# Two layers of cross attention on Trainium2: norm products in place, earlier first loads, clears shared out by layer, and a new order of the steps

## The reference

```python
# layer 0
text_out = softmax(q k^T / 4) v                  # q = x Wq, k and v from the 77 tokens
# four tokens ip = context[77:], none here: a softmax over no tokens adds nothing
x = text_out Wo + bo + x
# layer 1: text = context[:73], ip = context[73:77]
probs_t  = softmax(q k_t^T / 4)                  # over 73 tokens
text_out = probs_t v_t
qsem     = l2norm(probs_t @ text)                # 512 wide, for each head and query
sem      = qsem @ l2norm(ip)^T
fused    = q k_ip^T / 4 + 0.5 * sem
ip_out   = (softmax(fused) * spatial_mask) v_ip
x = (text_out + ip_out) W_out + b_out + x
```

## Time and profile before

| | |
|---|---|
| median of three runs | 2631.1 us (2628.68 to 2633.44) |
| the profiled execution | 2627.46 us, span 2625.7 us |
| busy share of the span | TensorE 89%, VectorE 66%, ScalarE 66%, GpSimd 60% |
| mean granted clock of TensorE | 0.976 of full |
| what ended last, by engine | TensorE 32%, DMA 15%, SyncE's queue 14%, ScalarE 10%, GpSimd 8% |
| first phase | 0 to 340.22 us |
| second phase | 340.22 us to the end |

### The profile page before, as it was taken

How to read it: one execution, slowest core, us unless ns; L and a number is a source line. 1 busy time by engine, 2 the same in 40 slices (tenths; PEclk the granted TensorE clock), 3 DMA queues, 4 the chain that set the end, 5 groups by cost and what they waited for, 6 DMA issues and landing times.

```text
span 2625.7 us, 90322 instructions
## 1 busy us (share of the span) xinstructions
PE 2329.1 (89%) x35896; PEld 1455.7 (55%) x35896; DVE 1724.0 (66%) x3053; ACT 1728.2 (66%) x2602; POOL 1580.1 (60%) x1055
## 2 busy tenths in 40 slices
PE   7899937989989999998999899999999999899984
PEld 5677724555555555555555555555555555555542
DVE  5533323777777777777777777777777777677764
ACT  3332315777777777777777777777777777777762
POOL 3121024666677666666666667777676666676663
PEclk9999968999999999999999999999999999999996
DMA  8667622343434433334334344334444343434331
GB/s 274 201 211 224 195 82 58 100 110 108 110 102 110 111 106 105 110 108 112 104 109 110 107 109 111 108 107 111 110 112 111 98 112 106 110 106 111 105 90 53
DMA packets 337021, 310.90 MB, mean 118 GB/s; under 512 B 179440, under 2 KB 280048, under 8 KB 336624
## 3 DMA queue, kind: packets, MB, share of 16 engines
q1 hardware_dynamic: 336624, 305.35, 41.6%
HBM read 164.66 MB, written 105.98 MB: 103 GB/s over the span
## 4 chain that ended last, share of the span: by engine, by line
PE 32%; DMA 15%; SPq 14%; ACT 10%; POOL 8%; issue 5%; DVE 3%; ACTq 0%; POOLq 0%; DVEq 0%
PE psum L927 12%; DMA rb<-r_dram 8%; DMA den<-ust 6%; SPq L854 6%; PE psum L1010 5%; ACT ef L1115 5%; PE psum L991 4%; POOL ust L1297 4%; PE psum L1024 4%; POOL al L1302 4%; SPq L861 3%; ACT ah L1153 2%; PE psum L930 2%; SPq L881 1%; ACT ust L1123 1%
## 5 line engine op out<-in xcount | busy, mean ns | idle before, releaser
L1115 ACT ACTIVATE ef<-psum 73x1024 f32<-73x1024 f32 (+1 forms) x640 | 636.9, 1015 | 266.1 <-PE psum L994 248.1
L1335 POOL TENSOR_TENSOR e<-ef,eh 73x1024 f32<-73x1024 f32 x320 | 681.9, 2131 | 81.5 <-ACT eh L1130 81.4
L1176 DVE TENSOR_REDUCE mneg<-psum 128x8 f16<-128x584 f32 (+1 forms) x640 | 464.2, 775 | 105.9 <-PE psum L959 91.5
L1198 DVE TENSOR_TENSOR wr<-psum,e 73x1024 f32<-73x1024 f32 x320 | 390.3, 1220 | 163.6 <-PE psum L1024 160.6
L991 PE MATMUL psum<-q_high,keys 32*73 32x256 f16 (+2 forms) x6144 | 323.8, 258 | 63.1 <-ACT ust L1123 32.0
L1010 PE MATMUL psum<-ef,values 128*32 128x256 f32 x5120 | 357.9, 388 | 4.4 <-DVE wr L1198 4.0
L1024 PE MATMUL psum<-eh,gram 128*73 128x512 f16 x1280 | 338.5, 387 | 12.9 <-ACT ef L1115 11.3
L1297 POOL TENSOR_TENSOR ust<-ust,rb 128x768 f32<-128x768 f32 x128 | 231.7, 1810 | 186.4 <-DMA rb<-r_dram 185.9
L1130 ACT ACTIVATE eh<-ef 73x1024 f16<-73x1024 f32 x320 | 315.6, 1045 | 0.0
L1123 ACT ACTIVATE ust<-psum 128x512 f32<-128x512 f32 x384 | 229.2, 597 | 122.7 <-PE psum L1010 121.9
L991 PEld LDWEIGHTS psum<-q_high,keys 32*73 32x73 f16 (+1 forms) x6144 | 187.6, 110 | 158.4 <-ACT ust L1123 45.5
(11 more groups left out here) (162 smaller groups left out, 4553.5 us busy)
## 6 DMA issues: line engine op xcount, KB each, us to landing
rb<-r_dram SPq DMA_DIRECT2D x128, 384.0 KB, 4.1
keys<-k_dram SPq DMA_DIRECT2D x128, 231.0 KB, 2.8
values<-v_dram SPq DMA_DIRECT2D x128, 192.5 KB
x<-in_x SPq DMA_DIRECT2D x64, 384.0 KB, 3.6
ust<-ust SPq DMA_DIRECT2D x512, 48.0 KB, 2.1
v_dram<-vst SPq DMA_DIRECT2D x16, 1280.0 KB
out<-outt SPq DMA_DIRECT2D x64, 320.0 KB, 3.2
k_dram<-kst SPq DMA_DIRECT2D x32, 616.0 KB, 4.0
```

Source lines behind the costliest of these rows:

```text
L1115: act.activation(ef[l][0:m, unit_heads(n), :].rearrange("t h s -> t (h s)"), src, ACT.Exp, scale=SM).then_inc(s_exp[l], 1)
L1176: dve.tensor_reduce(dst, o, AX_X, ALU.max, negate=True).then_inc(s_max[l], 1)
L1198: dve.tensor_tensor(wr[0:m, k % LOW_RING, :, :].rearrange("t (r h) s -> t r (h s)", r=2), banks(l, f"u{k}", 2)[0:m, :, :], e2[0:m, k % LOW ...
L1335: pool.tensor_tensor(e2[0:m, k % LOW_RING, :, :], ef[1][0:m, unit_heads(k), :], eh[0:m, unit_heads(k), :], ALU.subtract).then_inc(s_e2, 1)
```

## The change

1. **Norm products in place.** The tile `wr` is gone. `e2` has five buffers instead of three, and VectorE's `w` writes its product over the rest that it read. GpSimd's `b` for a batch waits for TensorE's `n` of the batch before (`f_n`), where it waited for `w` and a ring.
2. **First loads within the first phase.** The constants, the first input `x`, the layer 0 keys of batch 0 and the high and low parts of that input are made in the first phase, in tiles that both phases share (`Early`). To make room the raw projection weights take the place of `raw_v0` and `raw_v1`, and are loaded after the weights have been split.
3. **Stores of values in pieces.** Each of the five pieces of 128 (the last 104) rows is stored by itself as soon as it is ready, with one semaphore for each layer.
4. **Clears shared out by layer.** `all_ready` is gone. Small clears, clears for layer 0 and clears for layer 1 have a semaphore each, and only the steps of the first batch that need them wait.
5. **New orders.** All five lists of `ORDER`, and `USES`, are new.

```diff
+        small_clears, dve_clears, pool_clears = [mneg[0], mneg[1], va[0], va[1], gm], [ef[0]], [ef[1], eh, e2]
...
-        def all_ready(eng):
-
-            eng.wait_ge(s_zero, CLEARED)
-            eng.wait_ge(s_w, 16 * CONSTANTS)
...
             def weighted(l, b, k):
-                b.reached(dve, f_n, UNITS, k + 1 - LOW_RING if k >= LOW_RING else (4, 5, 3)[k] - UNITS)
                 b.reached(dve, s_e2, UNITS, k + 1)
                 b.reached(dve, f_u, UNITS, k + 1)
...
+                rest = e2[0:m, k, :, :].rearrange("t (r h) s -> t r (h s)", r=2)
+                dve.tensor_tensor(rest, banks(l, f"u{k}", 2)[0:m, :, :], rest, ALU.mult).then_inc(s_wr, 1)
...
             def rests(l, b, k):
-                b.reached(pool, s_wr, UNITS, k + 1 - LOW_RING if k >= LOW_RING else (4, 5, 3)[k] - UNITS)
+                b.reached(pool, f_n, UNITS, k + 1 - UNITS)
...
                 for l in both:
-                    results_of("v", l, 0)
-                    dst = v_dram[l][bass.DynSlice(token, full * P), :].rearrange("(k p) n -> p k n", p=P)
+                    for c, (k0, m) in enumerate(VT):
+                        wait_taken(sp, b, slot, KV_USES.index(("v", l, c, 0)))
+                        dst = v_dram[l][bass.DynSlice(token + k0, m), :]
...
+            for t, d in constants:
+                sp.dma_start(t[:], d).then_inc(s_const, 16)
+            sp.dma_start(early.xin[:], x[0:1, :, :, :].rearrange("a c p s -> p (a c) s")).then_inc(early.s_x, 16)
...
+            sp.wait_ge(s_kstored[0], 16 * KSTORES * 2 * (PAIRS - 1))
+            sp.dma_start(early.ke[:], k_dram[0][0:1, :, :].rearrange("a p n -> (a p) n")).then_inc(early.s_ke, 16)
...
             def exponentials(l, b, n):
+                if first(b):
+                    act.wait_ge(s_zero[l], CLEARED[l])
```

More of the change, by code:

```diff
@@ L1 @@
 from contextlib import ExitStack
+from dataclasses import dataclass
 import numpy as np
@@ L283, in keys_and_values @@
         s_kstored = [sem(f"keys_stored{half}") for half in (0, 1)]
-        s_istored, s_gstored, s_vstored = sem("ip_keys_stored"), sem("gram_stored"), sem("values_stored")
+        s_istored, s_gstored = sem("ip_keys_stored"), sem("gram_stored")
+        s_vstored = [sem(f"values_stored{l}") for l in both]
         s_ghigh = sem("gram_high")
@@ L317, in load_projection @@
             def load_projection(n):
+                sp.wait_ge(s_wl, len(order))
                 if n >= 2:
                     sp.wait_ge(s_pl, n - 1)
[L321 removed]
+                sp.dma_start(rawp[n % 2], projections[n][0].rearrange("(k p) n -> p k n", p=P))\
                   .then_inc(s_rawp[n % 2], 16)
@@ L401, in _ @@
             sp.wait_ge(s_last, 96)
+            sp.wait_ge(s_const, 16 * len(constants))
+            sp.wait_ge(s_keyless, 1)
             for half in (0, 1):
@@ L405, in _ @@
             sp.wait_ge(s_gstored, 16 * 2 * 2 * PAIRS)
-            sp.wait_ge(s_vstored, 16 * VSTORES * 2 * PAIRS)
+            for l in both:
+                sp.wait_ge(s_vstored[l], 16 * VSTORES * 2 * PAIRS)
         @block.tensor
@@ L656, in _, with attention @@
             pairs(pool, chunk)
-def attention(nc, psum, x, mask, bias, ident16_d, sel_d, pick_d, kmask_d, vmask_d, k_dram, v_dram, g_dram, c_dram,
-              kip_dram, vip_dram, r_dram, n_dram, s_dram, p_dram, wqs, wos, wqt, wot, rnorm, out):
+            pool.wait_ge(early.s_x, 16)
+            pool.tensor_copy(early.xh[:], early.xin[:]).then_inc(early.s_xh, 1)
+            pool.wait_ge(early.s_xh, 1)
+            pool.tensor_tensor(early.xl[:], early.xin[:], early.xh[:], ALU.subtract).then_inc(early.s_xl, 1)
+def attention(nc, psum, early, x, k_dram, v_dram, g_dram, c_dram, kip_dram, vip_dram, r_dram, n_dram, s_dram, p_dram,
+              wqs, wos, wqt, wot, rnorm, out):
     both = (0, 1)
@@ L690, in attention @@
         ql = [sb(f"q_low{l}", [P, PW], F16) for l in both]
-        ke = [sb(f"keys{l}", [P, 2 * CW * 2 * T], F16) for l in both]
+        ke = [early.ke, sb("keys1", [P, 2 * CW * 2 * T], F16)]
         va = [sb(f"values{l}", [P, H, SLOT]) for l in both]
@@ L807, in load_keys @@
             def load_keys(l, b, n):
+                if l == 0 and first(b):
+                    return
                 b.reached(sp, f_t[l], CW, 0)
@@ L812, in load_values @@
             def load_values(l, b, n):
+                if first(b):
+                    sp.wait_ge(s_small, SMALL)
                 b.reached(sp, f_a[l], CW, 0)
@@ L1167, in maxima @@
                 m = TXT[l]
+                if first(b):
+                    dve.wait_ge(s_small, SMALL)
                 b.reached(dve, f_m[l], 1, 0)
@@ L1279, in _ @@
         def _(pool):
+            for t in small_clears:
+                pool.memset(t[:], 0.0).then_inc(s_small, 1)
             for t in pool_clears:
-                pool.memset(t[:], 0.0).then_inc(s_zero, 1)
-            all_ready(pool)
+                pool.memset(t[:], 0.0).then_inc(s_zero[1], 1)
             def high_input(l, b, n):
+                if l == 0 and first(b):
+                    return
                 b.reached(pool, f_q[l], 1, 0)
@@ L1339, in _ @@
                                    "at": text_attended, "al": low_attended, "c": sem_values, "kb": ip_keys, "vb": ip_values, "b": rests})
+@dataclass
+class Early:
+    ident16: object
+    sel: object
+    pick: object
+    kmask: object
+    vmask: object
+    mask: object
+    bias: list
+    kip: object
+    xin: object
+    xh: object
+    xl: object
+    ke: object
+    s_x: object
+    s_ke: object
+    s_xh: object
+    s_xl: object
 def attention_stack_kernel(nc, x, ctx, ctxip, mask, wq, wk, wv, wo, bias, wk_ip, wv_ip, ident16_d, sel_d, pick_d,
```

139 lines of the change are left out of this document (67 added, 72 removed), and 16 rows, old and new, of the table USES.

## The result

The changed kernel takes 2531.36 us (median of four runs, 2517.18 to 2539.48) against 2629.89 us for the kernel before, measured beside it: a ratio of 0.9618, 95% interval 0.9573 to 0.9664. Measured once more (experiment 1), it gave 0.9597 (0.958 to 0.9613). The forecast was 2519 us, with a range of 2458 to 2588.

A forecast was written before the change was run, and what follows sets the result against it. It took a 33.97 us period, closed by the chain from denominators to 0o plus TensorE's work, as the bound. 91 us from 62 periods plus 21 at the boundary gave 112 us, so 2519 us, range 2458 to 2588.

The forecast's parts named there:

- Boundary: Between the two phases: earlier first projection and earlier block start together gain 21 us, bounds 18.2 to 22.2.
- that term: TensorE's clock after the boundary: a shorter gap could keep 2.4 GHz and save 6.5 us once; left out of the sum.
- Steady part: The loop over batches: the period falls from 33.97 to 32.5 us, bounds 31.5 to 33.6, 91 us over 62 periods.
- third cycle: TensorE's work alone in a period: 31.2 us, and nothing is faster than that.
- rival (a): TensorE becomes the only bound, the norm chain being shorter: period 31.5 us, time about 2457 us; chance 0.17.
- The jitter: Average period over the closely read one: 0.6 us before, 0.2 us added after, for a slow DMA partly covered by other chains.
- The small waits: TensorE's waits for two maxima and for the exponential, about 0.3 us each, beside the norm chain and not on top.
- First cycle: Denominators to 0o: 1.84 us of SyncE's queue leaves the chain, which falls from 19.35 to 17.6 us; whole cycle 31.5 us.
- Second cycle: Norms through DRAM, roots, 1o, w1 and VectorE's 0o: a 12.4 us chain against 11.3 of TensorE's work; binds at 32.3 us.
- (b): The new orders give nothing, only the boundary is won: period 33.9 us, time 2606 us; chance 0.09.
- my own case: Boundary gain plus a period of 32.5 us: 2519 us, own range 2463 to 2590; chance 0.69.
- (c): Slower: SyncE's queue becomes the bound through the input `x`; at a period of 34.7 us the time is 2655; chance 0.05.

The follow-up runs named there:

- experiments 2 and 3: The clamp of the norms written to PSUM and copied from there: in the changed kernel 2520.07 us (0.9567), in the kernel before a ratio of 0.9957.
- experiment 7: The kernel before with only SyncE's queue shortened, the stores and loads between the denominators' steps moved behind them: 2575.34 us against 2618.66, ratio 0.9833.
- experiment 6: The changed kernel with Gram matrix and key loads and the scores' store put back behind the inverses' stores on SyncE's queue: 2592.1 us, ratio 0.9835.
- experiment 10: The changed kernel with VectorE's 1o ahead of the roots and the clamp of the norms written to PSUM: 2583.51 us, ratio 0.9861 to the kernel before.
- experiment 11: The changed kernel with the clamp of the norms in PSUM and TensorE's 1a1 ahead of 1u2: 2527.73 us, ratio 0.9653 to the kernel before.
- experiment 5: The changed kernel with the five order lists and the bank order of the kernel before, everything else kept: 2612.36 us, ratio 0.9917.
- experiment 9: The changed kernel with VectorE's 1o ahead of the first root step instead of behind six: 2719.99 us, ratio 1.0321 to the kernel before.
- experiment 4: The changed kernel with the clamp of the norms as an instruction with two float32 inputs in SBUF: 2526.41 us, ratio 0.9576 to the kernel before.

## Why the prediction came out as it did

**Boundary: right.** 21 us forecast; the first projection comes 22.0 us earlier and the first read of 0o 20.6, since the way between the two takes 1.4 us longer. The block starts 2.9 us earlier (2.7 forecast, by the store in pieces), and the projection 0.2 us behind it (0 to 1.1). The three clears of GpSimd took 13.1 us beside other work, as forecast. VectorE's clear stands in the chain at 338.46 for 4.33 us, beside the projection, as the price said: the first `q_low`, ready to start when ScalarE ends `q_high` at 342.33, follows the clear at 342.70, so it cost 0.4 us at most. The clock averaged 0.58 and 0.66 instead of 0.50, so the shorter stand did not keep 2.4 GHz, and leaving that term out was right. The 6.5 us that I had worked out beside the Trainium skill, "TensorE: Matmul & The Clock Gate", Part 1, did not come in a size that the times show.

**Steady part: direction right, size a little off.** 1.47 us a period forecast (91 us in 62; there are 63), 1.21 measured (76.2 in 63). The forecast was 31.2 us of work and 1.3 of waits; it came to 30.73 and 2.03. Three terms were mis-sized and partly cancel:
- TensorE's own work. I took the same set of steps to mean the same busy time. The norm sums put together take 0.48 us less. The floor of 31.2, on which the third cycle and rival (a) rested, was not a floor. That the total still came out near is partly luck: this error and the next two pull opposite ways.
- The jitter. I added 0.2 us for it. The mean stands 0.35 over the median (32.74 and 32.39), and I had the wrong picture of its cause: not a slow DMA in one of several tight chains, but VectorE's clamp held up by GpSimd. It was already there in the kernel before, where the shortest and the longest clamp took 0.19 and 2.16 us; experiments 2 and 3 took it out in both kernels, for 8 and 11 us, through 0o in the one and through 0t0 in the other.
- The waits of a period without jitter. I had 1.1 us, by the norms' cycle alone; the median period has 1.66 (32.39 less 30.73). The small waits, which I took to lie beside that cycle and left out of the sum, are the larger part of it: the hand-offs below.

**First cycle: right for before, its new length not tested alone.** The wait for `al` went from 56.9 us to 11.5. That it bound the old period is shown by experiment 7. The forecast that it leaves the bound after the change holds too: even with 1.84 us of queue put back, `al` is waited for only 4 times. What I missed is that the edit of the queue works on both cycles: keys stood behind `rw`, and the norms hang on keys (experiment 6).

**Second cycle: the place right, the 12.4 us not met.** I named the norms as what binds, with 32.3 us. In short periods (32.2 to 32.4) 0o does not wait for it, but experiments 6 and 10 show how close it lies: what makes the roots or w1 late by 1.6 to 1.8 us costs 1.0 to 1.1 us a period. So it has, by an estimate from these two, some 0.5 to 0.8 us of slack, where I had laid it out at 1.1 us over TensorE's work. Where it touches TensorE was wrong as well: not at VectorE's 0o and 1u2 alone, but at the banks of 1o (filled by 0o) and of w1 (filled by 0t0).

**What binds instead** in a short period is a chain of hand-offs between TensorE and its readers: from the first scores through `mneg`, the exponential, 1o and 0o to 1u2. The chain of waits, one such stretch:

```profile
499.80 1.50 DVE mneg L1184 x2
...
501.35 0.32 PE psum L965 x8
...
503.64 1.02 ACT ef L1122
...
504.70 1.07 PE psum L1017 x16
...
509.60 2.78 PE psum L933 x24
...
512.50 0.97 DVE x L1277
...
513.51 1.05 PE psum L1033 x4
```

Each hand-off leaves TensorE 0.15 to 0.4 us without work and none is large. Summed from the trace over 59 periods, its idle time is 0.86 us a period ahead of the scores, 0.31 ahead of 0o (the long periods), 0.20 ahead of the turned scores, 0.19 of the Gram products, 0.18 of the sums of exponentials times values, 0.16 of the scores of the four tokens and 0.10 of the query projections. What taking one of them away would give is not shown; experiment 11 shows that moving one gives the wait to the next bank.

**Rivals.** (a) did not come: though TensorE's work fell, the waits stayed. (b) did not come: by experiment 5 the orders are worth 84 us. The time fell in my own case. (c) shows in traces of it: 0q waits for `xl` 11 times, 5.2 us in all, so that cycle is close but costs under 0.1 us a period.

## What to carry to other kernels

Put a removed wait's price by what binds next on each chain that passes through it: 1.84 us of queue gave 0.7 us a period alone and 1.0 with the other orders, since the same queue fed two cycles. Compare the median with the longest duration of each small VectorE line before laying out a period; where the longest is many times the median and ends with a GpSimd instruction, try its result in PSUM. Do it again after each new order, for an order alone took the stretched clamps from 15 to 61 of 64 (experiment 7). And look at where a small step's wait lies: here an order that put roots beside a long projection was worth 1.07 us a period over one that did 1o first (experiment 10).

## What the runs showed of the hardware

Some VectorE instructions with all operands in SBUF are held up for the rest of a GpSimd instruction in flight, and the profile books this as their own duration: the clamp's 0.19 us became up to 1.64 in the changed kernel, and 1.85 behind a 2.1 us product in experiment 9. In the long period shown, the clamp ends at 541.49 and `al` at 541.43. A tiny instruction is not spared: in the first phase one of 128x2 numbers takes 4.81 us (timelines of VectorE and GpSimd):

```profile
25.04 4.81 DVE L573 TENSOR_SCALAR pscale<-pmask 128x2 f32<-128x2 f32 x1
...
24.11 5.71 POOL L664 TENSOR_TENSOR cl<-cx,ch 128x2464 f16<-128x2464 f32 x1
```

Held up were a one-input float32 form (experiment 1) and a two-input form (experiment 4). Not held up were the clamp's neighbours of the same size that read or write PSUM, such as the product of root (in PSUM) and clamp, 208 to 221 ns in all 192 cases of the changed kernel, and the reciprocal in SBUF of experiment 4. The Trainium skill, "SBUF — State Buffer", section "SBUF: two separate sides", says that GpSimd and VectorE share one port pair as an exclusive lock, taken by whichever starts first, for VectorE's instructions in a two-port mode or with two inputs from SBUF (these only against a GpSimd instruction that reads SBUF), and that the other blocks fully. The traces agree for both forms of the clamp, if the one-input form ran in a two-port mode and the reciprocal did not; which mode an instruction ran in, no trace shows. What I had not expected is its reach: a 0.19 us instruction, stretched by 14.7 us in all in experiment 1, cost 8 us of one core's time through the bank of another step.

Matmuls of one kind are booked as less together: the 40 matmuls of a batch's norm sums took 3.05 us of TensorE's busy time in four places and 2.57 us in two. Ends of matmuls are modelled in this profile, so the split between true and booked time is open.

TensorE's clock fell in two experiments where it waited more: for 96 us of the time from 500 to 2400 us in experiment 9, with waits of 2.3 to 2.7 us ahead of 0t0, and for 31 us in experiment 6, with waits of up to 2.7 us. There it was granted 1.2 GHz; in the changed kernel and in experiment 10 it stayed at 2.4 GHz over the same time.
